# Three small VectorE steps placed later in the forward substitution of a gated delta-rule kernel

## What is computed

```
g = log(clip(sigmoid(h @ Wtg) * rho, 1e-6));  beta = sigmoid(h @ Wbeta)
for each token t, each mode m and head h:
    S  = S * exp(g_t)
    dv = (v_t - k_t @ S) * beta_t
    S  = S + outer(k_t, dv)
    o_t = q_t @ S                      # then mixed over modes, gated, @ Wo
x = x + ga * attention(layernorm(x) ...)
logits = layernorm(x) ... @ Wr + br    # router: top 2 of 8 experts, capacity 1024
x = x + gb * experts(...)              # two-layer MLP per expert
```

## Time and profile before

| | |
|---|---|
| time, median of 3 runs | 7000.74 us (6998.04 to 7004.32) |
| profiled execution, its own time | 6999.14 us |
| its span, first to last instruction | 6997.4 us |
| granted TensorE clock, mean | 0.817 |
| VectorE busy | 5135.8 us |
| TensorE busy | 4452.0 us |
| ScalarE busy | 3430.8 us |
| GpSimd busy | 2767.8 us |

### The profile page before, as it was taken

How to read it: one execution, slowest core, us unless ns; L and a number is a source line. 1 busy time by engine, 2 the same in 40 slices (tenths; PEclk the granted TensorE clock), 3 DMA queues, 4 the chain that set the end, 5 groups by cost and what they waited for, 6 DMA issues and landing times. The chain is left out here.

```text
span 6997.4 us, 195918 instructions
## 1 busy us (share of the span) xinstructions
PE 4452.0 (64%) x78513; PEld 3830.1 (55%) x78513; DVE 5135.8 (73%) x9800; ACT 3430.8 (49%) x6010; POOL 2767.8 (40%) x1789
## 2 busy tenths in 40 slices
PE   1666666666666666666666666666666666655993
PEld 1555555555555555555565555555555655553662
DVE  4888778888887887878888888778888888881003
ACT  1555555555555555555555555555555555542220
POOL 3444343444343443434443434434344443434003
PEclk6878878888887788888888787887878887887997
DMA  2000000000000000000000000000000000002223
GB/s 88 2 5 5 6 5 5 5 5 3 4 5 5 5 5 6 5 5 5 5 3 5 5 5 5 5 6 5 5 5 5 3 5 5 5 27 95 72 72 105
DMA packets 77479, 109.71 MB, mean 16 GB/s; under 512 B 20576, under 2 KB 66208, under 8 KB 75424
## 3 DMA queue, kind: packets, MB, share of 16 engines
q1 hardware_dynamic: 67616, 71.42, 3.2%
q0 software_dynamic: 8960, 25.39, 1.2%
HBM read 57.89 MB, written 38.89 MB: 14 GB/s over the span
## 5 line engine op out<-in xcount | busy, mean ns | idle before, releaser
L1573 POOL TENSOR_TENSOR state<-state,gc_end 128x512 f32<-128x512 f32 x512 | 591.5, 1172 | 1852.4 <-PE bank L595 1811.9
L589 PE MATMUL bank<-rhs,te 128*64 128x64 f32 x8192 | 412.6, 254 | 765.9 <-DVE rhs L1291 490.0
L572 PE MATMUL bank<-state,ke 128*64 128x64 f32 x16384 | 656.1, 248 | 341.0 <-DVE outT L1309 221.4
L572 PEld LDWEIGHTS bank<-state,ke 128*64 128x64 f32 x16384 | 616.8, 160 | 415.8 <-DVE state L1307 237.1
L797 ACT ACTIVATE te<-tt 32x256 f32<-32x256 f32 x1024 | 421.9, 412 | 802.6 <-DVE tt L1275 792.0
L589 PEld LDWEIGHTS bank<-rhs,te 128*64 128x64 f32 x8192 | 345.0, 163 | 844.4 <-DVE rhs L1291 795.8
L608 PE MATMUL last_two<-dvs,kte 128*64 128x64 f32 x16384 | 658.9, 241 | 180.1 <-DVE dvs L1298 180.1
L1272 DVE TENSOR_TENSOR last_two<-last_two,prod 128x31 f32<-128x31 f32 (+15 forms) x1984 | 692.4, 349 | 68.2
L847 ACT ACTIVATE ke<-kq 32x512 f32<-32x512 f32 x1024 | 642.9, 628 | 201.7 <-DVE kq L1223 188.0
L1270 DVE TENSOR_TENSOR prod<-bd,last_two 128x31 f32<-128x31 f32 (+15 forms) x1984 | 671.1, 338 | 68.3
L608 PEld LDWEIGHTS last_two<-dvs,kte 128*64 128x64 f32 x16384 | 597.2, 154 | 196.5 <-DVE dvs L1298 187.3
(11 more groups left out here) (257 smaller groups left out, 10221.1 us busy)
## 6 DMA issues: line engine op xcount, KB each, us to landing
w_sb<-in_L_ffn_W_dram SPq DMA_DIRECT2D x16, 1024.0 KB, 9.5
expert_rows<-ke SPq DMA_DIRECT2D x1, 8192.0 KB, 21.9
xrows<-expert_rows SPq DMA_DIRECT2D x16, 512.0 KB, 8.4
expert_outputs<-yrow POOLq DMA_DIRECT2D x16, 512.0 KB, 3.4
xt<-_attn_hidden_states_dram SPq DMA_DIRECT2D x32, 128.0 KB, 2.9
xr<-_attn_hidden_states_dram SPq DMA_DIRECT2D x32, 128.0 KB, 2.1
x_after_attention<-xr SPq DMA_DIRECT2D x32, 128.0 KB, 1.7
xo<-x_after_attention SPq DMA_DIRECT2D x32, 128.0 KB, 3.9
```

The source lines that it names most:

```text
L572: mm = pe.matmul(bank_mem[g][s, q % 4 * DK:q % 4 * DK + DK], ke[:, c, r, q, s], state[:, hh * HQ + q, r, :], start=(r == 0), stop=(r == 1))
L589: pe.matmul(bank_mem[g][s, q % 4 * DK:q % 4 * DK + DK], te[:, q, s], rhs[:, q, :], start=True, stop=True)
L1573: pool.tensor_tensor(sv, sv, gc_end[:, vh, 4 * g:4 * g + 4, c].unsqueeze(2).broadcast_to([P, 4, 2 * DK]), ALU.mult).then_inc(sem(f"state_f ...
```

## The change

Three keys of `meanwhile` are moved. The steps themselves, the order among them and everything on the other engines stay.

```diff
                 meanwhile = {}
                 if hh == 1 and not last:
-                    meanwhile.update({8: [lambda: clip_decays(n2)], 16: [lambda: sum_decays(n2)]})
+                    meanwhile.update({11: [lambda: clip_decays(n2)], 17: [lambda: sum_decays(n2)]})
                 if hh == 0 and not first:
-                    meanwhile[12] = [lambda: take_logits(n - 1)]
+                    meanwhile[24] = [lambda: take_logits(n - 1)]
                 solve(u, hh, first, meanwhile)
```

## The result

The changed kernel takes 6785.1 us (median of 4 runs, 6782.06 to 6788.35) against 7002.53 us (4 runs, 6998.04 to 7007.15) before: ratio 0.969, 95% interval 0.9673 to 0.9706, some 217 us less. The profiled execution took 6782.06 us with a span of 6780.4, so 217.1 us less than the profiled one of before.

What follows compares the result with a forecast made beforehand. VectorE, busy 73% of the span, was taken to bound the kernel, with its waits as the loss. Terms 202.5 + 25.2 = 227.7 us off 6999.1 gave 6771.4, stated as 6772 to match the median; range 6748 to 6800.

Steps and rivals of the forecast that it cites:

- the likeliest case: Whole kernel: the forecast itself, 6755 to 6790 us, given a chance of 0.68.
- The whole wait for the logits goes: First halves (hh = 0): take_logits at column 25 no longer waits in 31 loop executions, 202.5 us; the tail's 5.65 stays.
- No wait takes its place: TensorE's memory read (L572) still ends before right_sides (L1288) needs it, 1.3 us to spare in the worst tile; cost nothing.
- Clip and scan wait for GpSimd's running operation: Second halves (hh = 1): both hold VectorE until GpSimd's operation ends, then need at most 0.1 (clip) or 0.28 us (scan).
- The signs: Changed profile: clip 0.28 us in late kind, about 0.4 in early; scan about 1.0 and 2.3, ending 0.3 after L1538.
- a sign of being wrong: Second halves: the prediction is wrong if the clip takes about 2 us.
- part 2: Clip and scan moved in second halves: one column, 0.92 us, in 29 tiles, less 1.5 for two others: 25.2 us.
- early tiles: Second halves where L1538 ends 9.2 us after VectorE reaches the clip, against 10.4 in late ones; 16 early, 15 late.
- rival (b): Second halves: the clip loses the gap before L1535, ending them 1.3 us later in 16 tiles, 21 us: 6793; chance 0.09.
- Rival (a): TensorE's clock falls out differently: all early 6755, all late 6790, 6743 at best; chance 0.12 beyond the forecast's 6755 to 6790.
- a faster L589 after a shorter pause: TensorE's corrections: shorter idle might leave the clock higher, some 0.4 us a tile, 12 us more, 6743 at best.
- part 1: First halves: logits taken at column 25 instead of 13, removing VectorE's wait in 31 loop executions; 202.5 us.

Runs made afterwards that it cites:

- logits_30: The changed kernel, but with take_logits before the last column (31) instead of 25; ratio 0.9684 to the kernel before.
- psum_mask: The changed kernel, but the scan reads its restart mask from a copy in PSUM, leaving one SBUF input instead of two; ratio 0.9634 to the kernel before.
- scan_14: The changed kernel, but with the scan before column 15 instead of 18; ratio 0.9652 to the kernel before.

## Why the prediction was right, point by point

It said 6772 with 6748 to 6800; 6785.1 was measured, and the direction and the likeliest case were right.

- *The whole wait for the logits goes.* Right: 5.6 us are left, the tail's. Of the term of 202.5 us 198.0 came. Each hh = 0 substitution now takes 26.13 us, where the longer kind's 32.93 less the 6.94 of waiting were 25.99. The step that I priced at nothing is the one ahead of `take_logits`: the trace has a register operation of VectorE's queue on L1325 (64 ns) that forms the address, and the gap ahead of the instruction is 0.14 us where the columns have 0.03. It used to run inside the wait. 0.14 x 31 = 4.3 us. That it is this operation is read from the two traces, not tried.
- *No wait takes its place.* Right, with more room than I gave: I left 1.3 us in the worst tile, taking TensorE's gaps at the loop jump as possibly still to come when the wait ends. They were over by then. The read ends 3.4 to 4.5 us after the logits, not 7 to 8, and logits_30 shows 6 more columns of slack. TensorE's pause before L589, which I put at 2.4 or 5 us, is 6.46.
- *Clip and scan wait for GpSimd's running operation.* Right. psum_mask and scan_14 show it for the scan; for the clip it is read from where it ends. The signs came as named: the clip 0.28 us in late tiles and 0.28 to 0.55 in early ones, the scan 0.9 to 1.1 and 2.1 to 2.4, but for the two tiles in which the clip took the 1.9 that I had named as a sign of being wrong. By this the Trainium skill's rule of an exclusive lock ("SBUF — State Buffer", practical consequences) holds here to 0.3 us, and its statement that a VectorE instruction with two SBUF inputs contends with a GpSimd instruction that reads SBUF is borne out by 2.44 against 0.42 us for the same scan.
- *The gain of part 2 is one column a tile, 25.2 us.* The mechanism was right, early tiles went from 28.3 to 27.3 and late ones from 29.3 to 28.4; the sum was 21.4. The mis-sized piece is the mix: I kept 16 early tiles and 15 late, and it came out 11 and 20. With the old mix the new lengths would have given 28.6 us. Five more late tiles at 1.1 us each took 5.4 back, and two early ones that lost the clip's gap (rival (b), in 2 tiles instead of 16) at 0.9 us each 1.8. So that the sum came within 4 us of the term is two errors partly cancelling.
- *Rival (a)* was thus partly at work, to the worse side: fewer early tiles, not more. Its other piece, a faster L589 after a shorter pause, did not come: 1.12 us after 6.46 us of idle, as before.
- The 13 us between 6772 and 6785 are thus 4.5 of part 1, 3.8 of part 2, 1.4 in the setup, 0.9 in the gaps, and 2.4 of scatter: the profiled execution is the fastest of its four, 3.0 us under their median, where I had allowed 0.6. By my own figures (6771.4 and 1.6) that step should have been 1.6, and the forecast 6773.

What the forecast could not know from the rows is which tiles are early. The one before and the changed kernel give 16, 11 and, run again, 10; other placements give 8 to 31.

## What to carry to other kernels

A small step that stands in a serial chain of instructions belongs behind its inputs, not only its arithmetic: read when each input is there, and put the step past the latest case. Where VectorE and GpSimd work side by side, look at what GpSimd runs at the very moment at which a VectorE step with two SBUF inputs, or a `tensor_scalar`, would start; the step's duration is the rest of that operation plus a rest of its own (here 0.1 to 0.3 us), so it goes into GpSimd's idle stretch or takes one input from PSUM. And do not add up parts that were measured alone before looking at what else moved: clip and scan were worth 8 us by themselves, because the chain to the logits, for which VectorE still waited, ran its L490 at the lower clock in all tiles and came 0.9 us later in half of them; beside the moved logits, where nothing waits for that chain, they were worth 27 by the ratios (0.969 against 0.9729).

## What the runs showed of the hardware that I had not expected

- Filling a pause of 2.35 us of TensorE with 8 unread matmuls kept its clock at 2.4 GHz through the last gram and L544 in 31 of 31 tiles (2.09 and 3.72 us), against 11 and 10 tiles of the changed kernel without it; it was worth 0.3 to 0.4% of the kernel (0.9658 against 0.969 and 0.9702, on different chips) although TensorE is not the busiest engine. My reading is that it counts because ScalarE's sigmoid and copy, and with them GpSimd's operations, start by it; the clip and the scan then meet other operations of GpSimd.
- With 0.04 us of lead for GpSimd's L1535 the clip took 1.94 us, where it takes 0.28 when nothing holds it; the substitution got 0.9 us longer by it.
- On one chip the part behind the last substitution, with the same instructions, took 734.5 to 736.8 us in four kernels, and 710.5 to 715.7 in the other nine profiles, while the hh = 0 sums of the kernels with moved logits agreed to 0.2 us. Why was not tried.
